# One core, a decoder layer in fp32: tiles of x loaded one by one, last projections between transposes, second normalisation split

## The reference, cut to what matters

```python
x = x + attn(layernorm(x), Wq, Wkv, Wo, bo)        # 16 heads, 8 key heads, rotary, window and alibi bias
x = x + conv(ctx, ctx, layernorm(x), kern, D)      # long convolution of k*v, times q, 32 heads of 8
x = x + ffn(layernorm(x), ...)                     # shared MLP + 64 experts, top 6, capacity 128
```

## Time and profile before

| | us |
|---|---|
| median of 3 runs | 989.09 |
| lowest, highest | 983.96, 991.77 |
| the profiled execution | 995.12 |
| its span, first to last instruction | 993.3 |

### The profile page before, as it was taken

How to read it: one execution, slowest core, us unless ns; L and a number is a source line. 1 busy time by engine, 2 the same in 40 slices (tenths; PEclk the granted TensorE clock), 3 DMA queues, 4 the chain that set the end, 5 groups by cost and what they waited for, 6 DMA issues and landing times. The chain is left out here.

```text
span 993.3 us, 14608 instructions
## 1 busy us (share of the span) xinstructions
PE 901.2 (91%) x4947; PEld 626.9 (63%) x4947; DVE 551.3 (56%) x1143; ACT 232.5 (23%) x716; POOL 462.4 (47%) x512
## 2 busy tenths in 40 slices
PE   4899999998899999989999999998989799979980
PEld 3566666664677777766444586867666667666650
DVE  4688889767688888887888323222223122222220
ACT  1465646462400100122110021211111111111110
POOL 1545252634487888620272343444435244544422
PEclk9979999999999999999999999999999899999995
DMA  7300000020533333032007567898889789889863
GB/s 290 112 1 2 1 2 1 2 75 1 208 106 99 97 93 92 1 147 108 1 1 275 178 195 243 261 267 217 262 242 267 216 236 278 252 228 260 258 149 53
DMA packets 44142, 143.41 MB, mean 144 GB/s; under 512 B 7296, under 2 KB 11648, under 8 KB 35136
## 3 DMA queue, kind: packets, MB, share of 16 engines
q1 hardware_dynamic: 27424, 98.56, 27.0%
q0 software_dynamic: 14912, 37.76, 19.2%
q10 hardware_dynamic: 1760, 6.49, 1.7%
HBM read 114.36 MB, written 28.43 MB: 144 GB/s over the span
## 5 line engine op out<-in xcount | busy, mean ns | idle before, releaser
L1359 PE MATMUL ps<-arena 128*128 128x128 f32 (+4 forms) x2112 | 512.8, 401 | 10.1 <-DVE arena L812 5.7
L1359 PEld LDWEIGHTS ps<-arena 128*128 128x128 f32 x2112 | 337.9, 192 | 148.6 <-issue 103.7
L600 POOL DMA_INDIRECT out<-arena,scatter_rows x64 | 101.3, 1582 | 221.6 <-DMA out<-arena,scatter_rows 154.5
L1293 DVE TENSOR_TENSOR arena<-arena 128x256 f32<-128x256 f32 x64 | 27.3, 427 | 229.4 <-ACT arena L797 219.4
L1359 PE MATMUL ps<-features_T,arena 128*128 (+2 forms) x640 | 116.0, 338 | 0.0
L1359 PEld LDWEIGHTS ps<-features_T,arena 128*128 128x128 f32 x640 | 84.7, 188 | 37.3 <-issue 37.3
L650 ACT ACTIVATE arena<-ps 128x512 f32<-128x512 f32 (+1 forms) x137 | 78.5, 591 | 120.7 <-PE ps L1640 49.0
L472 POOL TENSOR_TENSOR arena<-arena 128x512 f32<-128x512 f32 x48 | 49.3, 1056 | 89.0 <-DVE arena L832 89.0
L797 ACT ACTIVATE arena<-ps 128x256 f32<-128x256 f32 x64 | 24.5, 383 | 264.6 <-PE ps L1359 245.4
L589 POOL DMA_INDIRECT arena<-token_rows,gather_rows x64 | 66.2, 1035 | 38.2 <-DVE gather_rows L1286 27.1
L660 ACT ACTIVATE arena<-arena 128x128 f32<-128x128 f32 x192 | 74.0, 389 | 16.7 <-DVE arena L820 16.7
(11 more groups left out here) (178 smaller groups left out, 1088.7 us busy)
## 6 DMA issues: line engine op xcount, KB each, us to landing
arena<-wexp SPq DMA_DIRECT2D x48, 1024.0 KB
residual<-wexp SPq DMA_DIRECT2D x16, 1024.0 KB
arena<-toeplitz_rows SPq DMA_DIRECT2D x32, 256.0 KB, 3.1
arena<-ctxE SPq DMA_DIRECT2D x32, 192.0 KB, 3.2
residual<-x SPq DMA_DIRECT2D x4, 1024.0 KB, 5.4
token_rows<-arena SPq DMA_DIRECT2D x16, 256.0 KB, 2.3
arena<-suT ACTq DMA_DIRECT2D x1, 2048.0 KB, 7.7
arena<-sdT ACTq DMA_DIRECT2D x1, 2048.0 KB, 12.6
```

The lines of the kernel that those rows point to most:

```text
L600: pool.indirect_dma_start(out, bass.IndirectOffsetOnAxis(ap=idxs[:, s % NY:s % NY + 1], axis=0), ysb[:, s % NY, :], None, compute_op=ALU.a ...
L1359: ins = TE.matmul(out_ap, lhsT, rhs, start=(n == 0), stop=(n == len(pairs) - 1))
```

## The change

Three things. SP loads the first four tiles of x by four DMAs with a semaphore each, and DVE waits for each tile ahead of its statistic; the counter raised at L377 is gone, and the loop over pairs 1 to 3 is written out. In the last pair PE's `first` 2 goes ahead of `probs_T(1, 0)`, "end" 0 between `probs_T(1, 0)` and `probs_T(1, 1)`, `first` 3 behind `attend(1)`; the fillers ahead of `probs_T(1, 1)` go; DVE's list follows this order, and it takes both halves of batch 0's attended values ahead of the second `inverse_sums`. The second normalisation is made in two parts: tiles 0 to 11 are aggregated and raised to the power ahead of the adds of "mid" and "end" 1, tiles 12 to 15 behind them; and the convolution of head 0 stands behind the transposes of tiles 0 and 1 instead of ahead of all, without fillers.

```diff
--- before.py
+++ after.py
@@ -218,6 +218,7 @@
         empt = [sem(f"bank{k}_drained") for k in range(NBANK)]
         w_loaded = sem("attention_weights_loaded")
         tables_loaded = sem("rope_bias_wo_loaded")
+        tile_loaded = [sem(f"x_tile{u}_loaded") for u in range(4)]
         x_loaded = sem("x_loaded")
         consts_ready = sem("consts_ready")
         small_loaded = sem("small_loaded")
@@ -316,15 +317,17 @@
             else:
                 rot(("first", 0), ("first", 1))
             rot(*[("pv", 0, c) for c in range(2)])
+            if not more:
+                rot(("first", 2))
             rot(*[("pT", 1, 0, q) for q in range(QB)])
+            if not more:
+                rot(("end", 0))
             rot(*[("pT", 1, 1, q) for q in range(QB)])
             if more:
                 prepared_fills("kqT")
-            else:
-                rot(("first", 2), ("first", 3))
             rot(*[("pv", 1, c) for c in range(2)])
             if not more:
-                rot(("end", 0), ("end", "mid"), ("end", 1))
+                rot(("first", 3), ("end", "mid"), ("end", 1))
 
         for part in ("xT", "qk", "kqT"):
             prepared_fills(part)
@@ -356,7 +359,8 @@
 
         @block.sync
         def _(sp):
-            sp.dma_start(X[:, 0:4, :], a["x"][0:4 * P, :].rearrange("(t p) d -> p t d", p=P)).then_inc(x_loaded, 16)
+            for u in range(4):
+                sp.dma_start(X[:, u, :], a["x"][u * P:(u + 1) * P, :]).then_inc(tile_loaded[u], 16)
 
             def load(dst, name, s):
                 sp.dma_start(dst, a[name]).then_inc(s, 16)
@@ -374,14 +378,13 @@
                 sp.sem_inc(s, 1)
             sp.sem_inc(scatter_landed, 5)
             sp.sem_inc(conv_done, 2)
-            sp.sem_inc(x_loaded, 16)
 
             sp.wait_ge(tables_loaded, 16 * 4)
-            with sp.Fori(1, PAIRS) as i:
-
-                sp.wait_ge(x_loaded, i * 16 + 16)
-                sp.dma_start(X[:, ds(i * 4, 4), :],
-                             a["x"][ds(i * (4 * P), 4 * P), :].rearrange("(t p) d -> p t d", p=P)).then_inc(x_loaded, 16)
+            for i in range(1, PAIRS):
+                if i > 1:
+                    sp.wait_ge(x_loaded, i * 16 - 16)
+                sp.dma_start(X[:, i * 4:i * 4 + 4, :],
+                             a["x"][i * (4 * P):(i + 1) * (4 * P), :].rearrange("(t p) d -> p t d", p=P)).then_inc(x_loaded, 16)
 
             sp.wait_ge(consts_ready, 1)
             sp.dma_start(out[T:ROWS, :], zeros[:]).then_inc(zero_written, 16)
@@ -528,8 +531,9 @@
             pair_products(0, 0)
             pair_products(1, 0)
 
-            pool.wait_ge(stats2_ready, 1)
-            G.tensor_tensor(rstd[:], rstd[:], minus_half[:], ALU.pow).then_inc(rstd2_ready, 1)
+            for k, tiles in enumerate((slice(0, NT - 4), slice(NT - 4, NT))):
+                pool.wait_ge(stats2_ready, k + 1)
+                G.tensor_tensor(rstd[:, tiles], rstd[:, tiles], minus_half[:, tiles], ALU.pow).then_inc(rstd2_ready, 1)
             last = SH // NTR - 1
             with pool.Fori(0, last) as i:
                 for s in range(NTR):
@@ -728,7 +732,8 @@
                 if more:
                     gate_exps(i + 1)
                 exps(1, 1, i)
-                attended(F, n, 0)
+                if more:
+                    attended(F, n, 0)
                 probs_T(F, n, 1, 0)
                 probs_T(F, n, 1, 1)
                 if more:
@@ -831,11 +836,11 @@
                 dve.wait_ge(exp_ready, i * 16 + (2 * b + c + 1) * 4)
                 V.reciprocal(rinv[:, b, 4 * c:4 * c + 4, :], rowsum[:, b, 4 * c:4 * c + 4, :]).then_inc(inverse_ready, 1)
 
-            def attended(F, n, b):
-                name = ("pv", b, 1)
+            def attended(F, n, b, c=1):
+                name = ("pv", b, c)
                 bank = F.bank(name)
                 dve.wait_ge(full[bank], F.filled(name, n))
-                V.tensor_copy(oT[:, 2:4, b * QB * 64:(b + 1) * QB * 64].rearrange("p r (q t) -> p r q t", t=64),
+                V.tensor_copy(oT[:, 2 * c:2 * c + 2, b * QB * 64:(b + 1) * QB * 64].rearrange("p r (q t) -> p r q t", t=64),
                               ps[:, bank, 0:QB * P].rearrange("p (q r t) -> p r q t", q=QB, r=2))\
                  .then_inc(empt[bank], 1)
 
@@ -900,8 +905,11 @@
 
             def ln1_stats(i):
 
-                dve.wait_ge(x_loaded, i * 16 + 32)
+                if i:
+                    dve.wait_ge(x_loaded, i * 16)
                 for u in range(4):
+                    if i == 0:
+                        dve.wait_ge(tile_loaded[u], 16)
                     V.bn_stats(stats1[:, u, :], X[:, ds(i * 4 + u, 1), :].rearrange("p t d -> p (t d)"))
                 V.drain()
                 for u in range(4):
@@ -1000,34 +1008,46 @@
                 probs_T(F, n, 0, 1)
                 scores_out(F, n, 1, 1)
                 inverse_sums(1, 0, i)
-                inverse_sums(1, 1, i)
                 if more:
+                    inverse_sums(1, 1, i)
                     query_gate(i + 1)
                     for m in range(3):
                         rotate(F, n, m)
+                    attended(F, n, 0)
+                    probs_T(F, n, 1, 0)
+                    probs_T(F, n, 1, 1)
+                    upper_keys(F, n)
+                    attended(F, n, 1)
+                    token_sums(F, n, i + 1)
                 else:
+                    attended(F, n, 0, 0)
+                    attended(F, n, 0)
                     first_rows(F, n, 0)
                     first_rows(F, n, 1)
-                attended(F, n, 0)
-                probs_T(F, n, 1, 0)
-                probs_T(F, n, 1, 1)
-                if more:
-                    upper_keys(F, n)
-                else:
+                    inverse_sums(1, 1, i)
+                    probs_T(F, n, 1, 0)
                     first_rows(F, n, 2)
+                    first_stats(F, n, 0)
+                    project(F, "end", 0, i)
+                    probs_T(F, n, 1, 1)
+                    ln2_stats(F, "end", 0, i)
+                    first_stats(F, n, 1)
+                    attended(F, n, 1)
                     first_rows(F, n, 3)
-                attended(F, n, 1)
-                if more:
-                    token_sums(F, n, i + 1)
-                else:
-                    for j in range(PAIRS - 1):
-                        first_stats(F, n, j)
-                    project(F, "end", 0, i)
+                    first_stats(F, n, 2)
+                    ln2_variances(0, NT - 4)
                     project(F, "end", "mid", i)
-                    ln2_stats(F, "end", 0, i)
+                    first_stats(F, n, i)
                     project(F, "end", 1, i)
-                    first_stats(F, n, i)
                     ln2_stats(F, "end", 1, i)
+                    ln2_variances(NT - 4, NT)
+
+            def ln2_variances(first, end):
+                V.drain()
+                for t in range(first, end):
+                    V.bn_aggr(meanvar[:, t, :], stats[:, t, :])
+                V.drain()
+                V.tensor_scalar(rstd[:, first:end], meanvar[:, first:end, 1], EPS, None, ALU.add).then_inc(stats2_ready, 1)
 
             ln1_stats(0)
             ln1(0)
@@ -1041,13 +1061,9 @@
             for i in range(PAIRS):
                 attention(FA[i], 0, i, i < PAIRS - 1)
 
-            V.drain()
             for t in range(NT):
-                V.bn_aggr(meanvar[:, t, :], stats[:, t, :])
-            V.drain()
-            V.tensor_scalar(rstd[:], meanvar[:, :, 1], EPS, None, ALU.add).then_inc(stats2_ready, 1)
-            dve.wait_ge(rstd2_ready, 1)
-            for t in range(NT):
+                if t in (0, NT - 4):
+                    dve.wait_ge(rstd2_ready, 1 if t == 0 else 2)
                 if t >= 4:
 
                     dve.wait_ge(full[FQ.bank(("x2T", t - 4))], FQ.filled(("x2T", t - 4)))
@@ -1367,8 +1383,8 @@
             def probs_T(F, n, b, c, i):
                 for q in range(QB):
                     bank = fill(F, ("pT", b, c, q), n)
-                    if q == 0 and b == c == 0 and i == 0 or q == 0 and b and i == PAIRS - 1:
-                        keep_clock(bank, 1 if c else 2)
+                    if q == 0 and c == 0 and (b == 0 and i == 0 or b and i == PAIRS - 1):
+                        keep_clock(bank, 2)
                     pe.wait_ge(prob_ready, i * 12 + ((2 * b + c) * QB + q + 1))
                     for g in range(4):
                         ins = TE.transpose(ps[:, bank, g * P:(g + 1) * P], prob[:, b, 4 * c + g, q, :], ident[:])
@@ -1511,18 +1527,19 @@
                     first_rows(F, n, 0)
                     first_rows(F, n, 1)
                 attend(F, n, 0)
+                if not more:
+                    first_rows(F, n, 2)
                 probs_T(F, n, 1, 0, i)
+                if not more:
+                    project(F, "end", 0, i)
                 probs_T(F, n, 1, 1, i)
                 if more:
                     qk_T(F, n, i + 1)
```

(14 more changed lines are left out.)

## The result

Over 14 runs each, the changed kernel has a median of 980.36 us (972.59 to 986.16) and the kernel before 986.88 (982.73 to 992.25). The ratio is 0.9933, 95% interval 0.9904 to 0.9963: 6.6 us faster (between 3.7 and 9.5), where 4.6 were forecast. The profiled execution took 984.94 us, its span is 982.7.

What follows compares the result with a forecast made beforehand. The prediction took PE, busy 91% of the span, as the bound. Gains of 2.4 + 2.2 = 4.6 us brought the profiled 995.12 to 990.5; carrying over the median's 6 us difference gave 984.5, range 977 to 990.

Steps and rivals of the forecast that it cites:

- Part 1: Loading x by tiles at the start: statistics end 3.1 us earlier, of which 2.4 us was taken as gain.
- The 0.7 that the sum took off for the clock: Dense projections at the start: gain taken as 2.4 us, between 1.5 and 3.1, because PE's clock may rise late.
- Part 2: Last pair, projections placed between the transposes: PE's last projection ends 3.7 us earlier.
- PE ended at 243.55: Last pair: end of PE's projections in the kernel before, against 239.85 predicted after the change, 3.7 us earlier.
- Part 3: Split second normalisation: starts 8.7 us earlier, but the convolution's 4.92 us come onto the path; 4.2 us gained while clock stays.
- The drop: PE's wait of some 3 us before the first transposes: the clock falls once, 2.0 us lost, leaving 2.2.
- No drop: Rival: PE's clock holds through the wait before the first transposes; gains 2.0 us more, 982.5; chance 0.21.
- Hidden load: Rival: at the start, tiles land together near 7 us or tables come late; 0.5 to 1.5 us gained, 986; chance 0.14.
- the rotation waiting for the tables: At the start: the rotations wait for tables, last landing at 18.3, and would start at 19.5 or later; margin 1 us.
- Low clock to the end: Rival: half clock from 242 through the second transposes; 11.2 us lost against 4.2 won, 993.7; chance 0.04.
- Loads in series: Rival: four tile loads at 3.1 us each in series, last landing at 13.1; 990.7; chance 0.03.
- The low stretch at 51.5 falls out: Rival: the half-rate stretch of PE work after 51.5 disappears; up to 4.7 us more gained, 979.8; chance 0.08.

Runs made afterwards that it cites:

- e3: Kernel before with only the last pair in the new order; normalisation, convolution and load of x as before: ratio to the kernel before 0.9949.
- e4: Changed kernel with x's first four tiles loaded in one DMA and the counter back: ratio to the kernel before 0.9989.
- e8: Kernel before with only the second normalisation split, 12 tiles ahead and 4 behind: ratio to the kernel before 0.9923.
- e11: Kernel before run again without any edit: last add 19.52 us and convolution loop 37.66 us behind the second inverse; no ratio given.
- e12: Kernel before with two fillers instead of one ahead of the second batch's last transposes: last add 17.83 us behind the second inverse; no ratio given.
- e1: Kernel before with only x's first four tiles loaded singly and the counter at L377 gone: ratio to the kernel before 1.0023.
- e5: Changed kernel with the convolution of head 0 ahead of all transposes, without fillers: ratio to the kernel before 0.9931.
- e6: Changed kernel with six filler matmuls in PE's wait ahead of the first transposes: ratio to the kernel before 0.9862, from 4 runs.
- e9: Changed kernel measured a second time, in another batch: ratio to the kernel before 0.9955.
- e10: Second measurement of e5, beside the changed kernel: ratio to the kernel before 0.9838, from 5 runs.
- e2: Kernel before with x's load still one DMA but with its own semaphore, without the counter: ratio to the kernel before 1.0020.
- e7: Changed kernel with x's first four tiles loaded in two DMAs of two tiles: ratio to the kernel before 0.9886.

## Why the prediction was right or wrong

**The sum.** 4.6 us were forecast, 6.6 (3.7 to 9.5) measured; the range 977 to 990 holds 980.36. The forecast of 984.5 stood on 989.09 for the kernel before, whose median over 14 runs is 986.88; 2.2 of the 4.1 us between 984.5 and 980.36 are that. Term by term:

- *Part 1, forecast 2.4 with 3.1 at the statistics.* The statistics ended 2.2 us earlier in the profile (7.75 against 9.97), and 2.1 to 3.7 earlier over six profiles: the fourth tile landed 0.9 later than the 6.14 that I took in this profile, and earlier in others. Averaged over the six profiles with x in one DMA and the counter (before, e3, e4, e8, e11, e12) and the six with single tiles (changed, e1, e5, e6, e9, e10), the projections start at 17.00 and at 14.10, 2.9 us earlier: 1.4 the counter (e2), the rest the tiles. The second inverse moves from 224.55 to 222.58, 2.0 us, uncertain by about 1, since either group scatters by 2.3 us and more. The 0.7 that the sum took off for the clock can't be confirmed. The 48 matmuls took 15.72 us in four of the six profiles with one DMA and in three of the six with tiles, and 17.6 to 18.1 in the others; whichever it is changes between two executions of one kernel (17.57 and 15.72 for before, 17.90 and 15.72 for e5 and e10).
- *Part 2, forecast 3.7.* The last add moved from +17.84 to +14.38, 3.5. "End 0" ran from 221.90 to 225.4 in PE's idle time, the inverse kept 0.81 us of slack. Against the other profiles of before's order and fillers (+19.5 in four of five) it is 5.1. This is the term that was mis-sized: **the step "PE ended at 243.55" of part 2 took the one profile of before as typical, and it was the good one.** That the range held in spite of it is in part luck. The prediction looked for a drop of the clock in the changed kernel and not for one in the kernel before, though the thin stretch of transposes with waits of 0.4 to 1.0 us stood in the timeline.
- *Part 3, normalising 8.7 earlier, conv on the path, 4.2 left.* Normalising starts at +16.61 for 16.2 predicted: 8.2 earlier. The convolution did come onto the path. Without the drop the gain of parts 2 and 3 is 35.88 - 31.32 = 4.6 (e6), for 4.2.
- *The drop, forecast 2.0.* It came, in all four profiles with this PE wait (changed, e4, e7, e9), and costs 1.55 (e6).
- So the loop starts 3.0 us earlier relative to the inverse than in the profile of before (2.2 forecast), and 4.8 earlier than in e11. With part 1's 2.0 that makes 5.0 or 6.8 us, and the timed differences are 6.6 and, in e9's batch, 4.4 us. The marks show the mechanism; the timings aren't fine enough to say which of the two sums holds.

**The rivals.** No drop: fell, in all four profiles with this wait. Hidden load (part 1 worth 0.5 to 1.5): the marks are against it, with 2.9 us at the projections and 2.0 at the second inverse, but only by a little, and e1's ratio doesn't exclude it; its mark, the rotation waiting for the tables, did appear and cost nothing. Low clock to the end: fell; it ended within the convolution. Loads in series: fell, the last tile was there by 7.06 in the changed kernel and by 7.22 in e10, not 13.1; the rule for loads of at least 1 MiB (the Trainium skill, "DMA: Bandwidth & Descriptors", Rules for kernel authors) is one on bandwidth, and here the order of arrival counted. The low stretch at 51.5 falls out: fell; windows from 46 to 62 us have a mean granted clock of 0.68 in the first profile of before and 0.79 in the other 13, that of e11 among them, which has no edit; so a part of it went by itself. The rule on gaps (the Trainium skill, "TensorE: Matmul & The Clock Gate", HAM oscillation) is for gaps longer than this wait of 2.95 us, so by it the drop needn't have come, and e11 shows one where no single wait was over 1.02 us. Nor does the length of the wait decide, as the prediction argued from the earlier trace rows: four transposes ran at full rate after 3.33 us in e10, where the granted clock stays 1.00 from there to 876:

```profile
869.96 0.66 PE L1655 MATMUL ps<-ident,arena 128*128 128x128 f32 x4 [3.33 <-DMA arena<-token_rows,gather_rows]
```

and at half rate after 2.48 us in e8:

```profile
761.76 1.11 PE L1646 MATMUL ps<-ident,arena 128*128 128x128 f32 x4 [2.48 <-DMA arena<-token_rows,gather_rows]
```

**What was missed.** The prediction saw that the convolution leaves the shadow and priced it, but didn't ask what the kernel would be without that step. e3 and e5 answer: the changed kernel reaches the loop 1.5 us later than part 2 alone and 3.6 later than the split with the convolution first. The drop of the clock is all of the first and 1.55 of the second.

## What to carry to other kernels

When a chain on one engine is shortened, look at what another engine did in its shadow: here 4.9 us of convolution belonged in PE's wait of 3 us, and putting it behind the first transposes gave away 3.6 us, 1.55 of them by the fall of the clock. Before one execution is used as the reference of a sum, ask which of its stretches at full clock were luck: transposes with waits of 0.4 to 1.0 us between them fell to half clock in four of five profiles. And where a kernel scatters by 1%, compare marks inside the profiles, relative to a common point, instead of totals.

## What the runs showed of the hardware

- The granted clock can fall without any long wait: transposes with waits of 1.02, 0.44 and 0.38 us between them came with a fall in e11. The same waits came with none in the first profile of before, and so did 0.17 us in place of the first in e12 (one profile).
- The length of a wait alone doesn't decide: transposes ran at full rate after 3.33 us in e10 and 2.76 us in before, and at half rate after 2.48 us in e8 and 2.70 us in before.
- It can rise on transposes alone, and does so in some executions only: with the same 16 transposes ahead, the 48 matmuls of the projections took 15.72 us in e11, full rate from the first, and 17.57 in the first profile of before, which is the same kernel. e11's row, beside the earlier trace rows:

```profile
17.12 15.72 PE L1359 MATMUL ps<-arena 128*128 128x512 f32 x48 [0.88 <-ACT arena L650]
```

- The 256 KB tiles of one load landed between 2.7 and 4.9 us after their issue in the changed kernel, between 2.7 and 3.5 in e5, and between 2.6 and 5.1 in e10, the same kernel as e5.
